# Attention written out for all quads; cross-attention's head, restack order and projection order changed, context split and norm on GpSimd

## The reference

```python
x = x + xattn(layernorm(x), ctx)   # 16 heads of 16, softmax over 256 context rows
x = x + attn(layernorm(x))         # 16 heads of 64, causal, 64 tokens
x = x + ffn(layernorm(x))          # 256 -> 1024 -> 256, gelu, weights and activations rounded to integers
```

## Time and profile before

| what | value |
|---|---|
| timed runs | 645.56, 646.29, 646.35 us; median 646.29 |
| profiled execution | 646.78 us, of which 644.8 are the span of its instructions |
| PE busy | 600.5 us, 93% of the span |
| DVE, ACT, POOL busy | 471.3, 386.7, 156.1 us |
| granted clock of PE, mean | 0.992 |

### The profile page before, as it was taken

How to read it: one execution, slowest core, us unless ns; L and a number is a source line. 1 busy time by engine, 2 the same in 40 slices (tenths; PEclk the granted TensorE clock), 3 DMA queues, 4 the chain that set the end, 5 groups by cost and what they waited for, 6 DMA issues and landing times. The chain is left out here.

```text
span 644.8 us, 18565 instructions
## 1 busy us (share of the span) xinstructions
PE 600.5 (93%) x6777; PEld 514.1 (80%) x6777; DVE 471.3 (73%) x982; ACT 386.7 (60%) x1016; POOL 156.1 (24%) x221
## 2 busy tenths in 40 slices
PE   6599999999999999889898999999999999799997
PEld 3598888888888898767697989898989898644587
DVE  4478788888788887768799666666666656677797
ACT  3488788888788888756332333333333333458895
POOL 6524233334242424000111212121212111260000
PEclk9799999999999999999999999999999999999999
DMA  6997767776867767824000000000000000000012
GB/s 202 256 265 182 187 163 182 175 182 167 192 154 187 168 161 207 237 68 140 1 3 2 2 0 0 0 0 0 0 0 0 3 1 2 3 1 1 0 50 83
DMA packets 37036, 58.43 MB, mean 91 GB/s; under 512 B 6912, under 2 KB 15232, under 8 KB 36992
## 3 DMA queue, kind: packets, MB, share of 16 engines
q1 hardware_dynamic: 29328, 42.75, 26.0%
q10 hardware_dynamic: 4592, 8.78, 4.9%
q0 software_dynamic: 3072, 6.30, 4.0%
HBM read 17.96 MB, written 2.10 MB: 31 GB/s over the span
## 5 line engine op out<-in xcount | busy, mean ns | idle before, releaser
L624 ACT ACTIVATE Pr<-pS,nmax 128x256 f32<-128x256 f32 x256 | 120.1, 484 | 26.7 <-DVE nmax L732 26.5
L732 DVE TENSOR_REDUCE nmax<-pS 128x2 f32<-128x512 f32 x128 | 87.5, 685 | 20.9 <-PE pS L468 19.5
L478 PE MATMUL pT<-ident,Pr 128*128 128x128 f32 x512 | 78.5, 276 | 3.4 <-DVE wraw L737 3.3
L966 POOL TENSOR_TENSOR a_Pr<-a_Pr,a_rinv 128x512 f32<-128x512 f32 x32 | 32.7, 1044 | 185.8 <-DVE a_rinv L1277 185.8
L468 PE MATMUL pS<-Kst,Qst 96*128 96x256 f32 x256 | 59.3, 314 | 11.9 <-DMA Qst<-QSl 6.8
L1147 ACT ACTIVATE a_Pr<-a_Pr 128x512 f32<-128x512 f32 x32 | 20.2, 631 | 76.0 <-DVE a_Pr L1269 76.0
L478 PEld LDWEIGHTS pT<-ident,Pr 128*128 128x128 f32 x512 | 60.0, 142 | 4.8 <-issue 4.4
L468 PEld LDWEIGHTS pS<-Kst,Qst 96*128 96x128 f32 x256 | 40.4, 194 | 21.1 <-ACT Pr L624 6.5
L624 ACT ACTIVATION_READ_ACCUMULATOR Pr<-pS,nmax 128x1 f32 x256 | 54.8, 214 | 0.0
L287 POOL DMA_DIRECT2D Qst<-QSh x60 | 30.2, 506 | 81.3 <-PE pS L468 56.3
L59 PE MATMUL a_pJ<-a_XTh,a_W1h 128*128 128x256 f32 x128 | 37.2, 290 | 2.5 <-DVE X L1290 1.6
(11 more groups left out here) (322 smaller groups left out, 1969.1 us busy)
## 6 DMA issues: line engine op xcount, KB each, us to landing
Kst<-WO_ints SPq DMA_DIRECT2D x96, 128.0 KB, 3.1
CT<-ctxT ACTq DMA_DIRECT2D x16, 512.0 KB, 4.8
Kst<-KSh SPq DMA_DIRECT2D x62, 128.0 KB, 2.9
Qst<-QSh SPq DMA_DIRECT2D x64, 64.0 KB, 2.5
Qst<-QSh POOLq DMA_DIRECT2D x64, 64.0 KB, 2.9
Kst<-KSl SPq DMA_DIRECT2D x31, 128.0 KB, 3.1
Qst<-QSl SPq DMA_DIRECT2D x32, 64.0 KB, 2.3
Qst<-QSl POOLq DMA_DIRECT2D x32, 64.0 KB, 2.9
```

Source lines behind the costliest of these rows:

```text
L478: last = pe.transpose(pT[s % 2][:, t, k, :], Pr[s % 2][:, t, P * k:P * k + P], ident[:, :])
L624: act.activation(Pr[c % 2][:, t, :], pS[c % 2][:, t, :], ACT.Exp, bias=nmax[c % 2][:, t:t + 1], accum_out=rsum[par][:, c // 4, 2 * (c % 4) ...
L732: dve.tensor_reduce(nmax[s % 2][:, :], pS[s % 2][:, :, :], AX.X, ALU.max, negate=True).then_inc(maxed, 1)
L966: pool.tensor_tensor(rows, rows, rinv[s][:, :].unsqueeze(2).to_broadcast([P, 8, SQ]), ALU.mult).then_inc(weighted, 1)
```

## The change

- Both attentions lose their hardware loops: every quad is written out, and semaphore counts become constants. Self-attention has no other change.
- The order of a quad's projections in cross-attention becomes X, Q, K, K after chunks 0, 2, 3, 4, then V, V after 6 and 7, V, V after 10 and 11, K, K after 12 and 14. Before it was X, K, K, Q after 0, 2, 3, 4; V, V; V after 10, K, K after 11 and 12, V after 14.
- SP issues Q's restack for the odd pair ahead of K's.
- The context's high part and the norm move to POOL; DVE and ACT lose them in the quads. In the head DVE makes the first two low parts.
- The head: X is loaded first, K's first part is followed by X, V of pair 1 is half projected ahead, the first restacks are spread over SP, ACT and POOL, and five filler products ahead of Q go.
- Feed-forward: the next group's transposes come after block 3 instead of 1, its high and low part after block 4 instead of 2.

```diff
-        AHEAD = [("K", 0, 0), ("K", 0, 1), ("X", 0, 0), ("Q", 0, 0), ("V", 0, 0), ("V", 0, 1), ("K", 1, 0), ("K", 1, 1)]
-        EVENTS = {0: (0, "X", 2, 0), 2: (1, "K", 2, 0), 3: (2, "K", 2, 1), 4: (3, "Q", 2, 0), 6: (4, "V", 1, 0),
-                  7: (5, "V", 1, 1), 10: (6, "V", 2, 0), 11: (7, "K", 3, 0), 12: (8, "K", 3, 1), 14: (9, "V", 2, 1)}
+        AHEAD = [("K", 0, 0), ("X", 0, 0), ("K", 0, 1), ("Q", 0, 0), ("V", 0, 0), ("V", 0, 1), ("K", 1, 0), ("K", 1, 1),
+                 ("V", 1, 0)]
+        def events_of(i):
+
+            p = 2 * i
+            if i == QUADS - 1:
+                return {6: ("V", p + 1, 0), 7: ("V", p + 1, 1)}
+            found = {0: ("X", p + 2, 0), 2: ("Q", p + 2, 0), 3: ("K", p + 2, 0), 4: ("K", p + 2, 1), 7: ("V", p + 1, 1),
+                     10: ("V", p + 2, 0), 11: ("V", p + 2, 1), 12: ("K", p + 3, 0), 14: ("K", p + 3, 1)}
+            if i:
+                found[6] = "V", p + 1, 0
+            return dict(sorted(found.items()))
...
-            body(0, False)
-            with eng.Fori(1, QUADS - 2) as i:
-                body(i, False)
-            body(QUADS - 2, False)
-            body(QUADS - 1, True)
+            for i in range(QUADS):
+                body(i, i == QUADS - 1)
...
-            load_w(W_ORDER[0])
             load_x(0, 2, x_in0)
-            for m in W_ORDER[1:]:
+            for m in W_ORDER:
                 load_w(m)
...
-            restack_first_k_high(sp, (0, 1, 2))
-            restack_first_k_low(sp, (0, 1, 2))
-            restack_first_q(sp, qst_sync[0], (0, 1))
-            restack_q(sp, qst_sync[1], 1, 3, 0, (0, 1))
+            restack_first_k_high(sp, kst_in[0], (0, 1))
+            restack_first_k_low(sp, kst_in[0], (0, 1))
+            restack_first_q_high(sp, qst_sync[0], (0,))
+            restack_first_q_low(sp, qst_sync[0], (0,))
+            restack_q(sp, qst_sync[1], 1, (0, 1))
...
-                    restack_k(sp, 1, EV0 + EV * i + 8, CHUNKS * (2 * i + 2))
-                    restack_q(sp, qst_sync[1], 1, EV0 + EV * i + 3, CHUNKS * (2 * i + 2), (0, 1))
+                    restack_q(sp, qst_sync[1], 2 * i + 3, (0, 1))
+                    restack_k(sp, 2 * i + 3)
...
+            def normalize(quad):
+                pool.wait_ge(ln_rs, quad + 1)
+                pool.wait_ge(proj, made("X", 2 * quad - 2))
+                for t in range(2):
+                    pool.tensor_scalar(XN[:, t, :], X[:, 2 * quad + t, :], mv[:, t, 0:1], rstd[:, t:t + 1],
+                                       ALU.subtract, ALU.mult).then_inc(ln_xn, 1)
+
+            def ctx_high(pair):
+                b = pair % 2
+                pool.wait_ge(ctx_in[b], 16 * (pair // 2 + 1))
+                if pair > 1:
+                    pool.wait_ge(proj, max(made("K", pair - 2, 1), made("V", pair - 2, 1)))
+                pool.wait_ge(ctx_hi, pair)
+                pool.tensor_copy(CS[b][HI][:, :, :], CT[b][:, :, :]).then_inc(ctx_hi, 1)
...
             def body(i, last):
-                if not last:
-                    ctx_low(0, 2 * i + 3)
+                if i == 0:
+                    ctx_high(2)
+                    ctx_low(2)
                 if two_ahead(i):
                     rstd_of(i + 2)
+                    normalize(i + 2)
                 if not last:
-                    restack_q(pool, qst_in[0], 0, EV0 + EV * i + 3, CHUNKS * (2 * i + 1), (2, 3))
-                    ctx_low(1, 2 * i + 4)
-                    restack_q(pool, qst_in[1], 1, EV0 + EV * i + 3, CHUNKS * (2 * i + 2), (2, 3))
-
-            steps(pool, body)
+                    restack_q(pool, qst_in[0], 2 * i + 2, (2, 3))
+                    ctx_high(2 * i + 3)
+                    ctx_low(2 * i + 3)
+                if two_ahead(i):
+                    ctx_high(2 * i + 4)
+                    ctx_low(2 * i + 4)
+                if not last:
+                    restack_q(pool, qst_in[1], 2 * i + 3, (2, 3))
+
+            steps(body)
...
-                if kind == "Q":
-                    spare(5)
...
-                    if s == 8 and not last:
-                        ctx_high(1, i + 2, EV0 + EV * i + 6)
-                    if s == 15 and two_ahead(i):
-                        ctx_high(0, i + 3, EV0 + EV * i + 10)
...
-                    if s == 8 and two_ahead(i):
-                        normalize(i + 2)
...
-                    if f == 1 and not last:
+                    if f == 3 and not last:
                         turn(g + 1)
...
-                    if f == 2 and not last:
+                    if f == 4 and not last:
                         x_high(g + 1)
```

More of the change, by code:

```diff
@@ L244, in ahead_bank @@
+        AHEAD_FREE = [0, 0, 0, 0, 0, 2, 1, 3, 5]
         def ahead_bank(r):
             flat = [t[:, :, :, :].rearrange("p t k q -> p (t k q)") for t in pT]
[L247 to L260, removed]
@@ L262, in steps @@
-        def steps(eng, body):
-            body(0, False)
-            with eng.Fori(1, QUADS - 2) as i:
-                body(i, False)
-            body(QUADS - 2, False)
-            body(QUADS - 1, True)
-        def two_ahead(i):
[L272 to L281, removed]
+            rows = pO[:, :, :, :, :].rearrange("p g b a q -> p (g b a q)")
@@ new lines, in cross_attention, with made, event, steps @@
+        EVENTS = [events_of(i) for i in range(QUADS)]
+        PLACE = {what: r for r, what in enumerate(AHEAD + [what for found in EVENTS for what in found.values()])}
+        def made(kind, pair, part=0):
+            return PLACE[kind, pair, part] + 1
+        def event(i, s):
+            what = EVENTS[i].get(s)
+            return what and (PLACE[what], *what)
+        def steps(body):
+            for i in range(QUADS):
+                body(i, i == QUADS - 1)
+        def two_ahead(i):
+            return i + 2 < QUADS
@@ L282, in restack_q, with k_landed, q_restacked @@
+        def k_landed(pair):
+            return RESTACK * (pair // 2 + 1) - (FIRST_BY_POOL if pair % 2 == 0 else 0)
+        def q_restacked(eng, pair):
+            eng.wait_ge(qst_sync[pair % 2], RESTACK // 2 * (pair // 2 + 1))
+            eng.wait_ge(qst_in[pair % 2], RESTACK // 2 * (pair // 2 + 1))
+        def restack_q(eng, done, pair, groups):
+            par = pair % 2
+            eng.wait_ge(lo, made("Q", pair - par))
             apart(eng, waited)
-            after(eng, scores, chunks_done)
+            after(eng, scores, CHUNKS * (pair - 1))
@@ L317, in restack_first_k_low, with restack_k @@
                 eng.dma_start(f32(Kst[0][64:96, jj:HP:4, :]),
-                              f32(KS[0][LO][32 * jj:32 * jj + 32, :, :])).then_inc(kst_in[0], 16)
-        def restack_k(eng, b, r, chunks_done, groups=range(4)):
-            after(eng, lo, r + 1)
+                              f32(KS[0][LO][32 * jj:32 * jj + 32, :, :])).then_inc(done, 16)
+        def restack_k(eng, pair):
+            b = pair % 2
+            eng.wait_ge(lo, made("K", pair, 1))
             apart(eng, waited)
-            after(eng, scores, chunks_done)
-            for jj in groups:
+            after(eng, scores, CHUNKS * (pair - 1))
+            for jj in range(4):
                 for u, part in enumerate((HI, HI, LO)):
@@ L430, in weights, with project @@
                 return [(W[HI][:, m, k, cols], W[LO][:, m, k, cols]) for k in range(KC)]
-            def project(r, bank, free, kind, part, pair, b, q_needs=None):
+            def project(bank, free, kind, pair, part):
+                b = pair % 2
                 after(pe, lo, free)
@@ L442, in project @@
                 elif kind == "Q":
[L443 removed]
+                    pe.wait_ge(lo, made("X", pair))
                     for g in range(2):
@@ L479, in turn, with weigh @@
                 last.then_inc(turned, 1)
-            def weigh(i, s, last):
-                par, b = s // 8 % 2, s // 4 % 2
+            def weigh(i, s):
+                pair, b = 2 * i + s // 8, s // 4 % 2
+                par = pair % 2
                 pe.wait_ge(pt_even, 8 * i + s // 2 + 2)
                 pe.wait_ge(pt_odd, 8 * i + s // 2 + 2)
+                pe.wait_ge(lo, made("V", pair, b))
                 if b == 0:
-                    first = isinstance(i, int) and i == 0
-                    pe.wait_ge(lo, EV0 + EV * i + (2 if last else 6) if par else 6 if first else EV0 + EV * i)
-                    after(pe, merged, 2 * i + par)
+                    after(pe, merged, pair)
                 for g in range(2):
@@ L525, in _ @@
             spare(10)
-            for r, (kind, ahead, part) in enumerate(AHEAD):
+            for r, (kind, pair, part) in enumerate(AHEAD):
                 if kind != "X":
                     pe.wait_ge(w_lo, W_ORDER.index("QKV".index(kind)) + 1)
-                if kind == "Q":
-                    spare(5)
-                project(r, ahead_bank(r), AHEAD_FREE[r], kind, part, ahead, ahead % 2, 3)
-            pe.wait_ge(lo, 6)
+                project(ahead_bank(r), AHEAD_FREE[r], kind, pair, part)
```

(11 more changed lines are left out.)

247 lines of the change are left out of this document (125 added, 122 removed).

## The result

The changed kernel takes 652.14 us (median of five runs, 651.07 to 654.59), the kernel before 646.26 beside it: a ratio of 1.0097, with a 95% interval of 1.0083 to 1.011. It is slower by 5.9 us, where I forecast 3.8 less, and lies above my range.

The account below looks back on a forecast made before the run. PE was taken to be full in every cross-attention quad. The terms -2.4 - 4.1 - 2.1 - 2.5 - 2.3 + 3.6 + 6.0 = -3.8 took 646.29 us to 642.5, range 635.5 to 648.

Parts of the forecast that it names:

- loops written out: Self-attention's loop: iteration 32.01 us against 32.03 for its written-out quad 6, so price 0.
- feed-forward: Next token group's transposes, moved two blocks later, no longer wait for DVE's rounding: -2.4 us, bounds -2.4 and 0.
- head and quad 0: Second score's wait -1.7, V projected ahead -1.5, quad 0's wait gone with the context split -0.9: sum -4.1 us.
- order and cast, quads 1 to 5: Quads 1 and 4 -2.1; ACT's cast 0.42 a quad; DVE's copy -2.3; second K projection's new wait +0.6 a quad.
- the even pair's restack: SP's restack starts about 2.9 us later, using up its slack; next quad's first score stalls 1.0 a quad: +6.0 us.
- Rival (b): Restacks bound the quads, both pairs waiting, 2.5 us a quad: sum +5.2, 651.5 us; chance 14%.
- My own signs of being wrong: Wrong if PE's first scores wait over 1.6 us in each quad, or DVE's queue never makes the second K projection wait.
- Rival (d): The head gains nothing and Q's wait costs 1 us a quad: 646.5 us; chance 8%.
- V ahead's 1.5: Head: V(1, 0), twelve matmuls, leaves quad 0 and fills PE's wait: -1.5 us.
- The new wait of the second K projection behind Q's low part: Second K projection needs the bank Q has just left: +0.6 us in six quads, +3.6.
- Rival (a): The even pair's restack stays hidden, so its +6.0 falls away: 636.5 us; chance 25%.
- Rival (c): POOL comes late with casts, norms and Q transfers, 0.5 us a quad more than forecast: 645.5 us; chance 8%.

Follow-up runs that it names:

- run 3: The kernel before with only the feed-forward's move (transposes after block 3, high and low part after block 4): 644.34 us, 0.996.
- run 1: The changed kernel with ACT's second context load of a quad (512 KB) issued after step 15 instead of 12: 644.72 us, 0.9962.
- run 11: The changed kernel with the even pair's Q restack ahead of its K restack on SP, load still after step 12: 644.18 us, 0.9963.
- run 13: The kernel of run 12 with V of pair 1 not projected ahead but made in quad 0 after chunk 6: 642.81 us, 0.9943.
- run 10: The kernel of run 1 with the context's high part on ACT again and GpSimd's odd Q restack ahead of the even pair's split: 648.8 us, 1.0033.
- run 4: The kernel before with its second context load of a quad issued after step 11 instead of 13: 646.52 us, 0.9996.
- run 5: The kernel of run 1 with DVE's row statistics at step 8 instead of 4 and GpSimd's norm behind the odd pair's context split: 641.21 us, 0.9926.
- run 9: The kernel of run 5 with quad 6's odd K projected after chunks 11 and 12 and its restack ahead of Q's on SP: 641.7 us, 0.9933.
- run 12: The changed kernel with the edits of run 1, run 5, run 9 and run 11 together: 641.94 us, 0.992.
- run 8: The kernel of run 1 with the quad's first context load also moved, from before step 3 to before step 5: 644.74 us, 0.9973.

## Why the prediction was wrong

The profiled executions' spans differ by +5.6 (644.8 to 650.4), against -3.8 forecast.

| step | forecast | measured (profiled executions) | from |
|---|---|---|---|
| loops written out | 0 | 0 in self-attention | its quads 32.02 and 32.03; in cross-attention not tested |
| feed-forward | -2.4 | -2.1 | first to last matmul of the first product, 32.98 to 30.86; run 3 |
| head and quad 0 | -4.1 | -0.9 | start of quad 1, 59.68 to 60.52, without the new wait of 1.7 |
| order and cast, quads 1 to 5 | -3.5 | -3.7 | run 1's quads, 160.25, against 163.95 |
| even restack, with what follows from it | +6.0 | +10.9 | 1.7 in quad 0; quads 1 to 5, 169.46 against run 1's 160.25 |
| quad 7 | 0 | +0.9 | to self-attention's first row maximum, 56.67 to 57.57 |

The rows sum to +5.1; the rest, 0.5, lies in small differences. (The row of quads 1 to 5 leaves out quad 6, which I had at +0.2 and which measured +0.1.)

The table sets single executions side by side, and run 1's is the fastest of its ten. By medians the stall with what follows from it is worth 7.4 (run 1) or 8.0 (run 11), 1.2 to 1.3 a quad, and without it those two kernels gain 1.8 and 2.3 on the kernel before, of which the feed-forward's move alone is 2.2 (run 3). So of the 7.6 us that I forecast for the head and the order together, 3.7 are there in the profiled executions (with quad 7's loss of 0.9 taken off) and next to nothing in the medians. The forecast failed on both sides: the stall was larger, and the gains were smaller.

**The step that failed is the even pair's restack**, by its size. The mechanism came as written: SP starts 2.7 us later in the quad (2.9 forecast), K's low part is written at 16.1 us (16.3), and the context load falls among the Q issues. I took 1.0 us a quad, between 0 and 1.9. Measured were 1.7, 0.8, 0, 2.5, 1.75 and 0 in quads 0 to 5 (the last interval between row maxima, less 2.13, its length where nothing waits). That is no small stall everywhere but one that is there or not: in quads 0, 3 and 4 the load was issued ahead of the last Q issue, in quad 1 0.13 us after it began, and in quads 2 and 5, without a stall, 1.15 and 0.4 us after. The lag of 5.5 us in quad 3 was longer than any that I had the earlier trace rows; those of 4.2 to 4.3 were not, and they made stalls too. I had counted the lag of before from the end of an issue (154.3); the view counts it from the start, so the last transfer landed at 153.77 and the slack was 3.1. The 2.7 us of lateness alone fit into that, as run 1 shows. And I let the stall end at the first score. The second odd K projection stands behind that score on PE, so the odd restack came late as well (in quad 2 PE waits 0.91 for its K), and two clock falls followed. All of it is 10.9 over six quads, 1.8 a quad, in the profiled executions. Rival (b) has almost the measured time, 651.5, but by another sum: it has both pairs' restacks waiting in every quad, 2.5 us, while in quads 1 to 5 the odd pair's K is waited for once, and the gains that did not come made up the rest. That its time fits is luck. My own signs of being wrong missed the failure: the first scores wait over 1.6 us in three quads of six, not in each, and the second K projection does wait, 0.13.

**The head** was mis-sized too, by 3.2 us. The second score did gain 1.2 of the forecast 1.7, but the first came 3.0 later, and the third, which needs the first's exponentials, 0.4 later: the wait moved from score 1 to score 2. I had followed one semaphore and not the chain behind it. Rival (d) has this half, a head that gains nothing. Of V ahead's 1.5, run 13 shows 0.4 to 0.9.

**The order** was right in sum in the profiled executions and wrong in one part. The waits for DVE's copy and for ACT's cast went, and so did the extra length of quads 1 and 4; the cast's wait is confirmed by run 10. That extra length was no fixed price: in the profiles of runs 3 and 4, whose cross-attention is that of before but for one load, quad 4 lasts 32.37 and quad 1 33.97 and 34.05. The new wait of the second K projection behind Q's low part, +0.6 a quad, is about 0.1 (PE stands 0.13 us ahead of it in quad 3). DVE's row maximum 6 does come 1 us later; in the profiled quads 3 and 4 PE has work for that time, but by the medians of run 5 it, or the norm, is not free. Rival (a), 636.5, is what the plan gives where the restack is hidden and the head gains; with the restack hidden and nothing else changed, runs 1 and 11 stand at 644.7 and 644.2, and with later statistics runs 5, 9 and 12 at 641 to 642. Rival (c) did not come: GpSimd's casts are in time, and its Q transfers land at 149.81 in quad 3, before SP's.

**The loops** I priced at 0 from self-attention, where the DMA engines are nearly idle (0.00 and 0.01). That says nothing of cross-attention, where they are busy 0.7 of the time. Written out, the program has more packets on the queue that the page calls instruction, before and after:

```profile
q8 instruction: 29, 0.48, 0.3%
```

```profile
q8 instruction: 54, 0.88, 0.6%
```

Before, quads 2, 3 and 5 hold none of these 16 KB packets and last 32.37 each, and the two long quads, 1 and 4, hold two and one; now each of them holds two or three. No run keeps the loop beside the rest of the change, so whether they cost time is not tested.

**Open.** What separates the executions of one kernel is not settled. Clock falls in quad 7 (in the profiles of runs 8, 9, 10 and 12) and a longer stretch at the lower level in the head (13.65 us instead of 10.24, in those of runs 10 to 13) both lower the mean clock, but the mean does not sort the times: in run 5 one execution at 0.989 took 641.22 and one at 0.992 took 642.67. The 3.5 us between the medians of 1 and 5 are not accounted for.

## What to carry to other kernels

Where a moved step uses up a slack to within the error of the estimate, don't price the middle: look for the transfer that will stand beside it after the move, and count a stall that is there or not, with the work that is queued behind the waiting instruction. This stall had two halves, lateness and a collision, and removing either was enough, so look for the cheaper one: here one load issued three steps later, or two lines on SP swapped. And a gain at one wait in the head counts only if the next instruction in the chain comes earlier too. Last, a table made from one profile for each kernel can flatter: set its sum beside the medians before you believe it.

## What the runs showed of the hardware

In the changed kernel's quad 3 a sixteenth of two transfers came late. The trace has sixteen semaphore increments for each transfer. Of the load's, fifteen had come by 158.78 and the last came at 160.34; of the Q transfer issued 0.26 us behind it, fifteen by 158.95 and the last at 160.53. Increments of the next two transfers of the same queue, issued at 156.58 and 157.13, came from 158.62 on, ahead of that last one. As the view counts their lag:

```profile
DMA to landing us min/median/max: 2.8/3.1/3.3
```

The Trainium skill (DMA: Bandwidth & Descriptors, Queues, rings and completion order) says that completion is not first in, first out for an issuing engine, and that a semaphore's increment lands only after every earlier write of that DMA engine, on any queue. The first agrees with these increments. The second would explain why the last increment of the transfer issued just behind the load comes 0.19 us after the load's last; no run here shows it by itself.

Between 153 and 161 us the view has one packet of the instruction queue, at 156.48, in the middle of the two transfers:

```profile
q8 instruction: 1, 0.02, 1.0%
```

1.0% of sixteen engines' 8 us is 1.3 us. The late sixteenths are 1.6 of the 2.5 us that quad 3 stalled; that this packet held them up is not shown, since the trace does not tell the DMA engines apart. The stalls of quads 0, 1 and 4 have no such packet between the load's issue and the last landing.

The norm was dearer on GpSimd than I had bounded it (0 to 1.04 us). The same operation on tiles of the same shape, in the changed kernel's groups of instructions (times, then busy in all and mean ns of one): on GpSimd, and on DVE, which still makes it in self-attention:

```profile
L406 POOL TENSOR_SCALAR XN<-X,mv,rstd 128x256 f32<-128x256 f32 x14 | 17.4, 1248 | 0.8
L1275 DVE TENSOR_SCALAR a_XN<-X,a_mv,a_rstd 128x256 f32<-128x256 f32 x16 | 5.8, 407 | 2.6 <-POOL a_rstd L133 2.5
```

That is a factor of 3.1. The subtraction that makes a context's low part, in the quads on GpSimd and in the head on DVE, differs by less:

```profile
L420 POOL TENSOR_TENSOR CS0l<-CT,CS0h 128x1024 fp32r<-128x1024 f32 x7 | 16.6, 2378 | 0.6
L805 DVE TENSOR_TENSOR CS0l<-CT,CS0h 128x1024 fp32r<-128x1024 f32 x1 | 1.2, 1226 | 0.9 <-ACT CS0h L681 0.9
```

The Trainium skill (GPSIMD Engine Reference, 8. Key points) has DVE about twice as fast for elementwise work. The subtraction agrees, with 1.9; for the norm the measurement decides. (The two rows that I set beside this rule in the prediction compare GpSimd with ScalarE, not with DVE.) PE does not wait for the norm in the changed kernel's quads 1 to 5.
